# Expert stage: TensorE enters a chunk's second products after six of eight activations

## The chip, the cores and the metric

The kernel runs on one core of one Trainium2 chip. The metric is the device time of one execution in microseconds (us). The time before is the median of three runs.

## What is computed

A graph network, a slice attention block, a hypergraph convolution and a mixture of experts are applied one after the other to 3125 nodes of 256 features, each added to its input. Only the last of them is touched:

```
logits = xt @ Wr + br
weights, top_idx = the two largest of softmax(logits), made to sum to 1
xe = xn[None, :, :] * ln_g[:, None, :] + ln_b[:, None, :]
h = jax.nn.gelu(jnp.einsum('end,edh->enh', xe, W1) + b1[:, None, :], approximate=False)
y = jnp.einsum('enh,ehd->end', h, W2) + b2[:, None, :]
out = (weights[:, :, None] * sel).sum(axis=1)
```

There are 8 experts, 256 features and a hidden width of 1024. `sel` are the outputs of a node's two experts.

## The kernel before, and its expert stage

The five engines run queues of their own and meet at semaphores. TensorE (PE) multiplies, ScalarE (ACT) applies the gelu, VectorE (DVE) scales and adds, GpSimd (POOL) issues the indirect transfers of rows, and SyncE (SP) issues the loads of weights.

**Chunks.** The pairs of node and expert are sorted by expert into 32 chunks: 24 of two units of 128 rows (256 rows) and 8 of one unit (128 rows). They are done in 8 turns of `TURN` = 4 chunks, three of two units and then one of one unit. Seven turns stand in a hardware loop (line 2475), where the values that semaphores are compared with are worked out in registers. The eighth is written out (line 2477) with constant values.

**What TensorE does for a chunk.** `turn_rows` (line 2431) transposes the gathered rows of the next chunk: four transposes for two units, two for one unit. `outputs` (line 2449) makes the second products of the present chunk. `hidden` (line 2439) makes the first products of the next chunk: 8 hidden blocks of 128 rows (`EK` = 8), each the sum of two matmuls, into PSUM banks 0 to 3 in turn. Each fp32 matmul shows as two weight loads (PEld) and two matmuls in the trace, so `hidden` is 32 of each, and `outputs` is 32 for two units and 16 for one. `turn_of_chunks` (line 2462) puts the three in the order `turn_rows`, `outputs`, `hidden`. The last chunk has no `turn_rows` before its `outputs`.

**The activations.** ScalarE (line 1057) reads each finished hidden block from PSUM, applies the gelu and writes block k of `hT`, then adds 1 to `e_gelu` (named `expert_gelus` where the order is shown). `outputs` loads block k of `hT` as the weights of product k, for k from 0 to 7, once for each unit i. `hidden` waits for `e_gelu` before it writes a bank again, at k = 4 to 7. The buffers `hT`, the weights `w1e` and `w2e` and the rows `xin` are double.

**Around it.** VectorE scales the transposed rows (line 1885, `xeT`) and later adds the bias and the gate to the output (lines 1893 and 1894), which adds 1 to `e_y`. GpSimd then adds the rows to `x_sum` by an indirect transfer (line 738) and gathers the rows of the chunk three further on (line 723, `xin`). SyncE loads W1 of the chunk two further on once all gelus of the present one are done (line 551), and its W2 (line 557) once the present output is made.

Line 2451 is the wait of `outputs` for the gelus:

```
pe.wait_ge(w2e_in[s], wi)
pe.wait_ge(e_gelu, gelu)
pe.wait_ge(e_y, y)
```

Of the kernel before, what the change touches and what calls it, by code (L numbers as in the profile page):

```python
# [61 lines left out]
EK = EH // P  # L62
# [44 lines left out]
def build(nc, x, src, dst, w, out):  # L107
    ctx = ExitStack()
    with ctx:
# [223 lines left out]
        def fresh(tag, *names):  # L333
            return [sem(f"{tag}_{n}") for n in names]
# [25 lines left out]
        e_tps, e_xe, e_hps, e_gelu, e_yps, e_y = fresh("expert", "transposed", "inputs", "hidden", "gelus", "outputs", "rows_out")  # L360
# [1550 lines left out]
        def _(pe):  # L1911
# [536 lines left out]

            def outputs(gelu, y, wi, s, n):
                pe.wait_ge(w2e_in[s], wi)  # L2450
                pe.wait_ge(e_gelu, gelu)
                pe.wait_ge(e_y, y)
                for i in range(n):
                    for k in range(EK):
                        ins = M(ps[:, 4 + s, i * F:(i + 1) * F], hT[s][:, k, i * P:(i + 1) * P], w2e[s][:, k, :], start=(k == 0), stop=(k == EK - 1))  # L2455
                ins.then_inc(e_yps, 1)

# [4 lines left out]
            def turn_of_chunks(g, last):  # L2462

                for j in range(TURN):
                    s, n, m = j % 2, UNITS_OF[j], UNITS_OF[(j + 1) % TURN]
                    final = last and j == TURN - 1
                    if not final:
                        turn_rows(rows_of(g, j + 1), 1 - s, m)
                    outputs(g * (TURN * EK) + (j * EK + EK + 1), g * TURN + (j + 1), g * (TURN * 16) + (j // 2 * 32 + 32), s, n)
                    if not final:  # L2470
                        hidden(g * (TURN * 2) + (2 * j + 4), g * (TURN * EK) + (j * EK + EK + 1), g * (TURN * 8) + ((j + 1) // 2 * 16 + 16), 1 - s, m)
# [28 lines left out]
```

## Time and profile before

| | us |
|---|---|
| median of three runs | 2862.1 |
| lowest and highest of them | 2860.65, 2863.26 |
| the profiled execution | 2860.8 |
| its span, first to last instruction | 2858.9 |
| TensorE matmul busy in the span | 2384.4 (83%) |

The profile comes from one execution of 2860.8 us, which is 1.9 us longer than its span and 1.3 us under the median. The expert stage fills the last 440 us of the span, from about 2419 us on. A timeline row has the start, the length, the engine with its line, the operation and how many instructions were merged; in square brackets stands how long the engine was idle before it and what the profile names as what ended that. "issue" means that the profile shows nothing it waited for. A weight load and its matmul overlap, and the ends of matmuls are modelled, so the rows of PEld tell best when TensorE goes on.

### The profile page before, as it was taken

The numbers are of one execution on the slowest core, as the hardware profiler recorded it, in microseconds if no ns is written. First come the engines' busy times: TensorE is split into PE (matmuls) and PEld (weight loads), VectorE is DVE, ScalarE is ACT, GpSimd is POOL, SyncE is SP. The second block draws the span as 40 slices with busy tenths as digits, with TensorE's granted clock in tenths as the row PEclk, the third lists the DMA queues.
The fourth block names the chain that finished last, engine by engine and source line by source line (L and its number), as shares of the span: only waits on it lengthen the run. The fifth ranks groups of instructions, "written<-read, shape, count | busy, mean of one in ns | idle before, by whom it ended". The sixth has DMA issues, their size and how long they took to land.

```text
span 2858.9 us, 39637 instructions
## 1 busy us (share of the span) xinstructions
PE 2384.4 (83%) x14320; PEld 1787.8 (63%) x14320; DVE 1037.8 (36%) x2746; ACT 450.0 (16%) x1221; POOL 881.8 (31%) x651
## 2 busy tenths in 40 slices
PE   5285553577859999999997888999999995999997
PEld 2151111345547776777774457888888895888886
DVE  7688885243321011112125745112220456111111
ACT  0030000000015000004104822000110002222222
POOL 6888888888830000000003410000000001333332
PEclk6595555798979999999999979999999996999999
DMA  9922223876460999990253000444344434667665
GB/s 338 311 1 0 0 1 63 236 207 184 68 192 0 215 224 243 238 246 0 81 165 107 1 1 1 138 147 133 124 143 154 158 124 147 192 200 216 198 202 171
DMA packets 298592, 397.88 MB, mean 139 GB/s; under 512 B 178133, under 2 KB 242028, under 8 KB 298410
## 3 DMA queue, kind: packets, MB, share of 16 engines
q1 hardware_dynamic: 115530, 268.24, 29.5%
q10 hardware_dynamic: 110560, 108.20, 14.3%
q0 software_dynamic: 72400, 20.05, 8.3%
q8 instruction: 67, 1.10, 0.2%
q14 instruction: 35, 0.29, 0.0%
HBM read 279.31 MB, written 99.82 MB: 133 GB/s over the span
## 4 chain that ended last, share of the span: by engine, by line
PE 63%; POOL 15%; DVE 7%; issue 6%; DMA 5%; ACT 1%; ACTq 1%; DVEq 0%; SPq 0%; POOLq 0%
PE ps L2045 14%; PE ps L2359 9%; PE ps L2361 9%; POOL odd_counts L617 7%; POOL at_counts L617 7%; PE ps L2455 7%; PE ps L2446 6%; PE ps L1971 4%; DMA odd_counts<-tarena 3%; PE ps L2063 3%; DVE late L1219 2%; PE ps L2292 2%; PE ps L2176 2%; PE ps L2315 2%; PE ps L2222 1%
## 5 line engine op out<-in xcount | busy, mean ns | idle before, releaser
L2359 PE MATMUL ps<-harena,ring 128*128 128x257 f16 (+1 forms) x2500 | 540.3, 272 | 5.1 <-DVE harena L1688 3.7
L2361 PE MATMUL ps<-harena,ring 128*128 128x256 f16 x2400 | 534.4, 271 | 0.0
L2045 PE MATMUL ps<-ring,harena 128*128 128x320 f16 (+1 forms) x3740 | 506.2, 297 | 1.4 <-ACT tarena L815 0.8
L2045 PEld LDWEIGHTS ps<-ring,harena 128*128 128x128 f16 x3740 | 366.8, 98 | 137.6 <-issue 3.1
L617 POOL DMA_INDIRECT at_counts<-harena x208 | 327.8, 1576 | 81.6 <-issue 78.3
L617 POOL DMA_INDIRECT odd_counts<-harena x208 | 330.1, 1587 | 66.7 <-issue 61.3
L1219 DVE SCALAR_TENSOR_TENSOR late<-ps,ring 128x512 f16<-128x512 f32 x416 | 287.4, 746 | 22.0 <-PE ps L1933 11.2
L1933 PE MATMUL ps<-harena,ident 104*128 104x512 f32 x208 | 186.6, 1014 | 116.3 <-DVE late L1219 115.3
L2359 PEld LDWEIGHTS ps<-harena,ring 128*128 128x128 f16 x2500 | 243.2, 97 | 40.1 <-DVE harena L1688 5.9
L2361 PEld LDWEIGHTS ps<-harena,ring 128*128 128x128 f16 x2400 | 232.2, 97 | 29.9
L685 POOL IOTA harena<- 1x32 int32 x1 | 0.2, 184 | 709.4 <-DVE xrows L1770 709.4
L2455 PE MATMUL ps<-ring,harena 128*128 128x256 f32 x896 | 201.7, 382 | 9.4 <-ACT harena L1057 5.2
L1933 PEld LDWEIGHTS ps<-harena,ident 104*128 104x128 f32 x208 | 50.3, 286 | 246.1 <-DVE late L1219 230.7
L2446 PE MATMUL ps<-harena,ring 128*128 128x256 f32 (+1 forms) x1024 | 201.7, 356 | 1.2 <-DVE harena L1885 1.2
L2455 PEld LDWEIGHTS ps<-ring,harena 128*128 128x128 f32 x896 | 167.6, 190 | 38.1 <-issue 16.5
L2446 PEld LDWEIGHTS ps<-harena,ring 128*128 128x128 f32 x1024 | 177.2, 192 | 22.3 <-issue 1.6
L2063 PE MATMUL ps<-feat,wl 128*128 128x320 f32 x448 | 130.4, 452 | 63.9 <-DVE feat L1301 47.0
L738 POOL DMA_INDIRECT x_sum<-harena x56 | 88.8, 1586 | 267.3 <-DVE harena L1894 227.5
L1057 ACT ACTIVATE harena<-ps,harena 128x256 f32<-128x256 f32 (+1 forms) x256 | 114.6, 448 | 310.1 <-PE ps L2446 302.1
L786 ACT ACTIVATE bn_k<-bn_k 128x4 f32<-128x4 f32 (+1 forms) x3 | 0.6, 204 | 1026.7 <-DMA at_counts<-ring 620.5
L2063 PEld LDWEIGHTS ps<-feat,wl 128*128 128x128 f32 x448 | 88.0, 199 | 104.5 <-issue 50.1
L1301 DVE SCALAR_TENSOR_TENSOR feat<-ps,sc,late 128x640 f32<-128x640 f32 x30 | 26.5, 884 | 340.6 <-PE ps L2045 340.6
(410 smaller groups left out, 2486.3 us busy)
## 6 DMA issues: line engine op xcount, KB each, us to landing
ring<-at_counts SPq DMA_DIRECT2D x145, 800.0 KB
ring<-L_ffn_W SPq DMA_DIRECT2D x64, 1024.0 KB, 5.2
ring<-ad_counts SPq DMA_DIRECT2D x50, 800.0 KB
at_counts<-tarena ACTq DMA_DIRECT2D x5, 4000.0 KB, 21.8
odd_counts<-tarena ACTq DMA_DIRECT2D x5, 4000.0 KB
ad_counts<-xrows ACTq DMA_DIRECT2D x25, 800.0 KB, 7.8
xrows<-odd_counts SPq DMA_DIRECT2D x20, 800.0 KB
at_counts<-ring ACTq DMA_DIRECT2D x20, 800.0 KB
```

Source lines behind the costliest of these rows:

```text
L617: nc.gpsimd.indirect_dma_start(out=table, out_offset=bass.IndirectOffsetOnAxis(ap=eidx[:, c:c + 1], axis=0), in_=evalue[:, c:c + 1], in_of ...
L738: nc.gpsimd.indirect_dma_start(out=x_sum, out_offset=bass.IndirectOffsetOnAxis(ap=to_row[:, j:j + 1], axis=0), in_=yrow[c % 2][:, i, :], i ...
L1057: nc.scalar.activation(hT[s][:, k, 0:n], ps[:, k % 4, 0:n], ACT.Gelu, bias=evc[s][:, k:k + 1]).then_inc(e_gelu, 1)
L1219: ins = V.scalar_tensor_tensor(out=ejunk[q], in0=ps[:, LOOK + s, :], scalar=ekey[:, bass.ds(g + q, 1)], in1=eweight[:, GE - P - q * P:2 * ...
L1933: M(ps[:, LOOK + g % LOOK, :], ident[0:ER, g:g + 1].to_broadcast([ER, P]), ekeyT, start=True, stop=True).then_inc(keys_spread, 1)
L1971: ins = M(ps[:, 4 + n % 4, 0:c], weights[:, d, fo * P:(fo + 1) * P], feat[:, d, h * HB:h * HB + c], start=(d == 0), stop=(d == 3))
L2045: ins = M(ps[:, 2 * f + h, 0:c], part[:, t, (2 * k + f) * P:(2 * k + f + 1) * P], chunk[q][:, s, h * HB:h * HB + c], start=(t == 0 and par ...
L2063: ins = M(ps[:, k + h, 0:HB], wl2[:, d, fo * P:(fo + 1) * P], feat[:, d, h * HB:(h + 1) * HB], start=(d == 0), stop=(d == nfi - 1))
L2359: ins = M(ps[:, i, 0:wide], lhs, hh[:, t, 0:wide], start=(t == 0), stop=(t == T - 1))
L2361: ins = M(ps[:, i, 0:F], lhs, hl[:, t, :], start=False, stop=False)
L2446: ins = M(ps[:, k % 4, 0:n * P], w1e[s][:, d, k * P:(k + 1) * P], xeT[s][:, d, 0:n * P], start=(d == 0), stop=(d == 1))
L2455: ins = M(ps[:, 4 + s, i * F:(i + 1) * F], hT[s][:, k, i * P:(i + 1) * P], w2e[s][:, k, :], start=(k == 0), stop=(k == EK - 1))
```

## The change

`outputs` no longer asks for all eight gelus of its chunk before its first product. It asks for six, and then, in the first unit's pass alone, for the seventh before product k = 6 and for the eighth before product k = 7. The products, their order and their operands are the same. `gelu` counts all eight, so `gelu - EK + 1 + k` is `gelu - 1` at k = 6 and `gelu` at k = 7.

```diff
             def outputs(gelu, y, wi, s, n):
                 pe.wait_ge(w2e_in[s], wi)
-                pe.wait_ge(e_gelu, gelu)
+                pe.wait_ge(e_gelu, gelu - 2)
                 pe.wait_ge(e_y, y)
                 for i in range(n):
                     for k in range(EK):
+                        if i == 0 and k >= EK - 2:
+                            pe.wait_ge(e_gelu, gelu - EK + 1 + k)
                         ins = M(ps[:, 4 + s, i * F:(i + 1) * F], hT[s][:, k, i * P:(i + 1) * P], w2e[s][:, k, :], start=(k == 0), stop=(k == EK - 1))
                 ins.then_inc(e_yps, 1)
```

The other engines' instructions are the same. On TensorE, in the loop, this is the third chunk of a turn, after the two transposes for the chunk of one unit. A row is an instruction, with the semaphores that it waits for; REGISTER_ALU works out a value in a register, and may carry a wait itself.

```order
 L2451 REGISTER_ALU [waits expert_W2_in0]
 L2452 REGISTER_ALU [waits expert_gelus]
-L2455 MATMUL ps<-ring,harena 128x256 [waits expert_rows_out]
-L2455 MATMUL ps<-ring,harena 128x256 x15
+L2457 MATMUL ps<-ring,harena 128x256 [waits expert_rows_out]
+L2457 MATMUL ps<-ring,harena 128x256 x5
+L2456 REGISTER_ALU
+L2457 MATMUL ps<-ring,harena 128x256 [waits expert_gelus]
+L2456 REGISTER_ALU
+L2457 MATMUL ps<-ring,harena 128x256 [waits expert_gelus]
+L2457 MATMUL ps<-ring,harena 128x256 x8
```

The wait at the entry stays and asks for a smaller value, and two waits and two register computations stand between the 6th and the 8th product (in two of the four chunks of a turn it is one computation). On TensorE in the turn that is written out, from the end of `hidden` of the last chunk to the end of the stage, before:

```order
 L2446 MATMUL ps<-harena,ring 128x128 [waits expert_gelus]
 L2446 MATMUL ps<-harena,ring 128x128
 L2455 MATMUL ps<-ring,harena 128x256 [waits expert_rows_out,expert_gelus,expert_W2_in1]
 L2455 MATMUL ps<-ring,harena 128x256 x7
```

and with the change:

```order
 L2446 MATMUL ps<-harena,ring 128x128 [waits expert_gelus]
 L2446 MATMUL ps<-harena,ring 128x128
 L2457 MATMUL ps<-ring,harena 128x256 [waits expert_rows_out,expert_gelus,expert_W2_in1]
 L2457 MATMUL ps<-ring,harena 128x256 x5
 L2457 MATMUL ps<-ring,harena 128x256 [waits expert_gelus] x2
```

Here no register is worked out, and the two further waits sit on the last two products.

## Rows read from the trace of the kernel before

**Rows 1.** The page: the span, and the last chain by engine.

```profile
span 2858.9 us, 39637 instructions
...
PE 63%; POOL 15%; DVE 7%; issue 6%; DMA 5%; ACT 1%; ACTq 1%; DVEq 0%; SPq 0%; POOLq 0%
```

**Rows 2.** Windows: stretch, length, busy time by engine, granted clock, DMA share, GB/s.

```profile
2530.00:2585.00 55.00, 53.83 (x269) 47.04 (x268) 8.72 (x16) 15.92 (x36) 19.63 (x15) 1.00 0.73 216
```

**Rows 3.** Waits of weight loads from 2420 us: who for whom, total, times, longest.

```profile
PEld ps L2455 <- issue: 16.5, 31, 0.7
...
PEld ps L2436 <- DMA harena<-xn_rows,harena: 0.6, 1, 0.6
```

**Rows 4.** Timeline, entry of `outputs` after four transposes, a chunk of two units.

```profile
2534.72 0.57 PEld L2436 LDWEIGHTS ps<-ident,harena 128*128 128x128 f32 x4
...
2535.20 0.48 ACT L1057 ACTIVATE harena<-ps,harena 128x256 f32<-128x256 f32 x1 [0.39 <-PE ps L2446]
...
2535.80 0.19 PEld L2455 LDWEIGHTS ps<-ring,harena 128*128 128x128 f32 x1 [0.50 <-issue]
2535.80 0.48 PE L2455 MATMUL ps<-ring,harena 128*128 128x256 f32 x1 [0.27 <-ACT harena L1057]
```

**Rows 5.** Timeline, entry after two transposes, a chunk of two units.

```profile
2460.33 0.47 ACT L1057 ACTIVATE harena<-ps,harena 128x256 f32<-128x256 f32 x1 [0.39 <-PE ps L2446]
...
2460.93 0.30 PEld L2455 LDWEIGHTS ps<-ring,harena 128*128 128x128 f32 x2 [0.71 <-issue]
```

**Rows 6.** Timeline, entry after four transposes, the chunk of one unit.

```profile
2471.77 0.37 ACT L1057 ACTIVATE harena<-ps,harena 128x128 f32<-128x128 f32 x1
...
2472.26 0.30 PEld L2455 LDWEIGHTS ps<-ring,harena 128*128 128x128 f32 x2 [0.39 <-issue]
```

**Rows 7.** Timeline, the last chunk, and the last addition of rows.

```profile
2835.74 1.71 ACT L1057 ACTIVATE harena<-ps,harena 128x128 f32<-128x128 f32 x4
...
2837.52 3.32 PEld L2455 LDWEIGHTS ps<-ring,harena 128*128 128x128 f32 x16 [0.72 <-issue]
...
2842.44 1.55 POOL L738 DMA_INDIRECT x_sum<-harena  x1 [3.88 <-DVE harena L1894]
```

**Rows 8.** Timeline, the second turn's start, where the gathered rows come late.

```profile
2482.99 0.47 ACT L1057 ACTIVATE harena<-ps,harena 128x256 f32<-128x256 f32 x1 [0.39 <-PE ps L2446]
2483.06 0.42 PEld L2436 LDWEIGHTS ps<-ident,harena 128*128 128x128 f32 x4 [0.57 <-DMA harena<-xn_rows,harena]
...
2483.59 0.30 PEld L2455 LDWEIGHTS ps<-ring,harena 128*128 128x128 f32 x2
```

**Rows 9.** Timeline, weight loads of whole `outputs` and `hidden` groups.

```profile
2519.94 3.76 PEld L2446 LDWEIGHTS ps<-harena,ring 128*128 128x128 f32 x32
...
2535.80 6.77 PEld L2455 LDWEIGHTS ps<-ring,harena 128*128 128x128 f32 x32 [0.50 <-issue]
...
2542.59 6.88 PEld L2446 LDWEIGHTS ps<-harena,ring 128*128 128x128 f32 x32
```

**Rows 10.** Timeline of SP and POOL at a turn's end: loads and gather.

```profile
2522.01 0.37 SPq L557 DMA_DIRECT2D ring<-L_ffn_W  x1
...
2525.32 0.29 SPq L551 DMA_DIRECT2D ring<-L_ffn_W  x1
...
2527.28 0.99 POOL L723 DMA_INDIRECT harena<-xn_rows,harena  x1 [0.30 <-issue]
...
2529.35 0.37 SPq L557 DMA_DIRECT2D ring<-L_ffn_W  x1
```

**Rows 11.** Windows: the ten microseconds around that gather.

```profile
2525.00:2535.00 10.00, 10.00 (x48) 8.75 (x47) 1.30 (x3) 3.32 (x7) 4.28 (x4) 1.00 1.03 326
```

**Rows 12.** The last chain in order of time: the late rows of the second turn.

```profile
2475.09 7.94 DMA harena<-xn_rows,harena
```

**Rows 13.** The page, DMA issues: out, in, count, KB each, median us to landing.

```profile
ring<-L_ffn_W SPq DMA_DIRECT2D x64, 1024.0 KB, 5.2
```

**Rows 14.** The page, groups: instructions, count, busy us, mean ns, idle before.

```profile
L2455 PE MATMUL ps<-ring,harena 128*128 128x256 f32 x896 | 201.7, 382 | 9.4 <-ACT harena L1057 5.2
```

## The prediction

> **What bounds the kernel now.** I read the page first. The span is 2858.9 us, and the chain that ended last lies on TensorE for 63% of it [rows 1]. The change touches the last 440 us alone, so the next view is the busy time by stretch. From 2530 to 2585 us matmuls are busy 53.83 of 55 us, the granted clock is 1.00, the upper of the two levels (2.4 GHz), and the DMA engines are busy 0.73 of the time [rows 2]. TensorE sets the pace there, and what it idles is worth its full length, since the tail after it (output, addition, store) is released by it.
>
> The third view is the list of waits. TensorE's weight loads of `outputs` waited 31 times, 16.5 us in all [rows 3]. The profile puts this down to "issue", so it names no cause. The timeline of one entry gives it. The four weight loads of the transposes start at 2534.72 and end at 2535.29. The eighth gelu runs from 2535.20 to 2535.68. The first weight load of `outputs` starts at 2535.80, after 0.50 us idle and 0.12 us after the gelu's end [rows 4]. The same 0.12 to 0.13 stands in the other forms: gelu end 2460.80, load 2460.93, idle 0.71 [rows 5]; gelu end 2472.14, load 2472.26, idle 0.39 [rows 6]. Even where the transposes themselves came late, the gelu ends at 2483.46 and the load starts at 2483.59 [rows 8]. In the written-out turn, with no register to work out, it is 0.07 (2837.45 to 2837.52) after an idle time of 0.72 [rows 7]. So the eighth gelu is what every entry waits for. It is short of cover: it ends about 0.6 us after `hidden`'s last product, and four short transposes fill only part of that.
>
> **Part 1, the entry wait falls from eight gelus to six.** Gelus of a chunk of two units follow each other every 0.87 us (0.48 busy, 0.39 idle) [rows 4], so the sixth ends 1.73 us before the eighth, at about 2533.95. That is 0.8 us before the transposes begin. In a chunk of one unit four gelus take 1.71 us [rows 7], 0.43 each, so the sixth of the last chunk ends at about 2836.59, and 0.07 later is 2836.66, still before the 2836.80 at which its load group has ended (2837.52 less 0.72). So the entry wait no longer ends last anywhere. What does is TensorE's own queue. The other two entry waits, W2 and the output buffer, aren't near: the tightest W2 is issued at 2522.01 and read at 2535.80, 13.8 us later [rows 10, 4], against a median landing of 5.2 us [rows 13] and the 7.94 us of the late rows [rows 12]. The output buffer was freed a chunk ago.
>
> Taken back: the 31 idle times, **16.5 us** [rows 3]. Four transposes' loads start 0.11 us apart and last 0.14 (0.57 us for four whose first step is 0.22) [rows 4]. A next load would thus start some 0.03 us before the last one's end, which adds 31 x 0.03, **0.9 us**.
>
> **Part 2, two new waits per chunk.** Behind each stands everything TensorE has left to do, and VectorE's output addition waits for the end of it. Product 6 is the 13th weight load of `outputs`. At 0.216 us each (31 steps and 0.19 in 6.88 us [rows 9]) it comes 2.6 us after the entry. With the entry at about 2535.27 that is 2537.9, and the eighth gelu ends at 2535.68 [rows 4]: 2.2 us of cover, worth nothing saved or lost while the gelus keep their pace. If that cover were gone, each us that a gelu ends later would cost a us. For one unit the margin is the same 2.6 us less at most 0.7 [rows 7].
>
> What does a wait that is already satisfied cost in the middle of a stream? `hidden` has four of them in each group, most with a register computation, and no step shows: 32 loads in 6.88 us at 256 columns, and 32 in 3.76 us at 128, where there would be least to hide them behind. The group `outputs`, with no wait inside, took 6.77 us, which is 0.11 less, but its second load comes 0.11 early because the first had waited [rows 9]. So the lower bound is zero. The upper bound for a wait is 0.05 us, the difference between the two lags after the gelu (0.12 with a register computation, 0.07 without) [rows 4, 7]: 64 x 0.05 = 3.2 us. I take **zero**, because `hidden` is the same pattern on the same engine.
>
> The seam itself: does TensorE go from the last transpose to the first product without a pause when the waits are satisfied? From `outputs` to `hidden`, also past register computations and two waits, it does: the one group ends at 2542.57 and the next starts at 2542.59 [rows 9]. If the 0.12 us of a released wait stayed at each entry, 32 x (0.12 + 0.03) = 4.8 us would be lost. I take none, and keep it for the range.
>
> **Part 3, what is late next: the rows of a turn's second chunk.** They are gathered at the turn's end, beside two 1 MB weight loads, with the DMA engines at 1.03 of their time and 326 GB/s [rows 10, 11]. The gather starts at 2527.28 and its rows are transposed at 2534.72, 7.44 us later [rows 10, 4]. In the second turn they needed 7.94 us [rows 12], and the transposes waited 0.57 us, the only such wait [rows 3]. It cost nothing then, since the gelu came last anyhow. Between that gather and those transposes lies one entry, that of the chunk of one unit, so the room falls by 0.39 + 0.03 = 0.42 us to 7.02. In the second turn the rows are then the bound. The load that now starts at 2483.59 could start 0.11 after the transposes' last, at 2483.45, which is 0.14 us sooner [rows 8]. From gather to `outputs` it gains 0.14 where the other terms counted 0.42 (the entry itself had no idle time in the 16.5): **-0.3 us**. For the six other turns I only know that the rows took at most 7.44 us. Some may need more than 7.02, the more so as the next W2 (issued 2529.35 [rows 10]) starts 0.42 us sooner and shares the engines. Bounds: 0, or 0.42 in each, 2.5 us. I take **-0.3 us**, one late turn.
>
> **The sum.** 16.5 + 0.9 - 0 - 0.3 - 0.3 = 16.8 us. The profiled execution would go from 2860.8 to 2844.0, and the median from 2862.1 to **2845.3 us**, 0.6% less. A measurement of this kernel can tell about 0.2%, 5.7 us, from no change. The end of the span moves with TensorE, since the last addition of rows was released by the last output (its idle time of 3.88 us ended with VectorE) [rows 7].
>
> **A page that speaks against it.** The Trainium skill (Advanced Engine Details and Errata, section Network/Comms) says that reading a semaphore from the sequencer takes 50 to 100 ns on trn2. If each of the 64 new waits paid that on TensorE's path, an estimate from that page, 3.2 to 6.4 us of the gain would go, and the sum would be 10.4 to 13.6. `hidden`'s even steps [rows 9] speak against it; it is rival 2 below.
>
> **The rivals.**
>
> 1. *The rows come late in every turn.* For: in the second turn it is so already, and the DMA engines are full there [rows 11, 12]. Against: in six of seven turns nothing waited for rows [rows 3]. Price: if all seven need 7.94 us, each turn has only 0.14 of the 0.95 us that it could have between gather and `outputs` (0.42 and 0.53). The sum without any lateness is 16.5 + 0.9 + 0.5 = 17.9, less 7 x 0.81 = 5.7: 12.2 us, **2849.9**.
>
> 2. *A satisfied wait costs 0.05 us in mid-stream*, by the difference of the lags [rows 4, 7]. 16.8 - 3.2 = 13.6 us, **2848.5**. Against it stand the steps of `hidden`.
>
> 3. *Each new wait empties TensorE's pipeline.* After a real wait the first matmul shows 0.48 us, where the mean over all of them is 0.38, so about 0.10 is lost beside the lag of 0.12 [rows 4, 14]. 64 x 0.22 = 14.1 us, leaving 2.7: **2859.4**, which is within 0.2%. Against: again `hidden`, and that the gelus are done 2.2 us before.
>
> 4. *The change doesn't do what it says.* "issue" could mean that TensorE's own queue needs the 0.5 us for three register computations, and the gelu's end falls beside it by chance. Then nothing is gained, and 0 to 3.2 us of new computations are lost: **2862.1 to 2865.3**. Against: the idle time is 0.39, 0.50 and 0.71 by form while the distance to the gelu stays at 0.12 [rows 4 to 6], and the 0.72 stands where no register is worked out [rows 7].
>
> 5. *Slower: a W2 load gets in front of the gathered rows.* Place: the turn's end. W2 of the turn's second chunk is issued 2.07 us after the gather now [rows 10] and 0.42 sooner with the change. Its 1 MB at 326 GB/s [rows 11] is 3.2 us, which the rows would land later in each of seven turns. 17.9 - 7 x 3.2 would be -4.5 us, and with the 0.42 us less room up to -7.4: **2866.6 to 2869.5**. It decides from rows that need 7.0 + 3.4 = 10.4 us, because only then are 7 x 3.4 us lost, the whole 17.9 and the 5.7 of a visible loss. The longest seen is 7.94 [rows 12].
>
> **How the numbers follow.** Forecast 0.78, rival 1 0.08, rival 2 0.05, rival 3 0.03, rival 4 0.03, rival 5 0.03. Faster by over 0.2% are the forecast and rivals 1 and 2: 0.91. Within 0.2% are rivals 3 and 4: 0.06. Slower: 0.03. The range takes in the forecast and rivals 1 and 2. Its low end is the sum without lateness, 2862.1 - 17.9 = 2844.2, less the 1.4 us by which the lowest run lies under the median: 2842.8. Its high end is rival 1 at 2849.9, about what the 4.8 us of a lag at each entry would give too (2850.1), with a little of the runs' spread: 2850.8.
>
> **What the changed profile would show.** Right: the 16.5 us of waits before `outputs`' weight loads gone or under 1 us; the first load of `outputs` 0.03 us before the transposes' last one has ended; `outputs` in even steps of 0.216 us past the 12th load; a turn of about 50.0 us instead of 52.2 (2483.59 to 2535.80 [rows 8, 4]); the eighth gelu ending inside `outputs`. Part 3 shows as waits of the transposes for gathered rows, once or twice, at the start of a turn. Wrong: a step over 0.25 us at the 13th or 15th load (rivals 2 and 3), an entry that still starts 0.12 us after something (the seam), or waits for rows in every turn (rivals 1 and 5).

## The result, and the profile after

| | before | after |
|---|---|---|
| first six runs of each, median | 2862.7 us | 2844.0 us |
| ratio, 95% interval | | 0.9927 (0.9897 to 0.9956) |
| later set, 12 runs against 35, median | 2863.1 us | 2845.8 us |
| ratio, 95% interval | | 0.9940 (0.9917 to 0.9964) |
| profiled execution | 2860.8 us | 2842.3 us |
| its span | 2858.9 us | 2840.5 us |

The kernel is faster by 0.6 to 0.7%. The forecast was 2845.3 us, which is 0.6%. The first ratio, set against the 2862.1 us from which the forecast started, gives 2841.2 us, which is 1.6 us below the low end of the stated range. The medians of those same runs are only 18.7 us apart, and the median of after and the later ratio (2844.9 us) lie inside. Both intervals are wide: the later one stands for 10.3 to 23.8 us, which holds the forecast and rival 1 alike. So the runs' times show that the kernel is faster, and the profiles have to show why. What was wrong is taken up behind the experiments.

The page of after, and its busy time by stretch, answer to [rows 1, 2, 11]. TensorE's matmuls are now busy 55.00 of 55 us, where it was 53.83.

```profile
span 2840.5 us, 39679 instructions
PE 64%; POOL 16%; issue 6%; DVE 6%; DMA 5%; ACTq 1%; ACT 1%; DVEq 0%; SPq 0%; POOLq 0%
```

```profile
2530.00:2585.00 55.00, 55.00 (x280) 48.94 (x279) 9.72 (x18) 14.77 (x33) 20.02 (x17) 1.00 0.76 219
2520.00:2530.00 10.00, 10.00 (x49) 8.76 (x48) 1.61 (x4) 3.31 (x7) 4.56 (x4) 1.00 1.02 325
```

The waits of weight loads from 2420 us on, which answer to [rows 3], are down to a single row. It is the first `hidden` of the stage, which also stood there before. The 16.5 us before `outputs` are gone.

```profile
PEld ps L2446 <- issue: 1.6, 1, 1.6
```

The timeline of after (line 2457 is the product that was line 2455) shows the entries that answer to [rows 4 to 8]: behind four transposes and behind two, the chunk of one unit, the last chunk, and the starts of the first and the second turn.

```profile
2529.62 0.58 PEld L2436 LDWEIGHTS ps<-ident,harena 128*128 128x128 f32 x4
2530.10 0.47 ACT L1057 ACTIVATE harena<-ps,harena 128x256 f32<-128x256 f32 x1 [0.39 <-PE ps L2446]
2530.16 6.78 PEld L2457 LDWEIGHTS ps<-ring,harena 128*128 128x128 f32 x32
...
2458.12 0.36 PEld L2436 LDWEIGHTS ps<-ident,harena 128*128 128x128 f32 x2
2458.45 0.73 PEld L2457 LDWEIGHTS ps<-ring,harena 128*128 128x128 f32 x4
2458.60 0.47 ACT L1057 ACTIVATE harena<-ps,harena 128x256 f32<-128x256 f32 x1 [0.39 <-PE ps L2446]
...
2468.85 0.81 ACT L1057 ACTIVATE harena<-ps,harena 128x128 f32<-128x128 f32 x2
2469.36 0.52 PEld L2457 LDWEIGHTS ps<-ring,harena 128*128 128x128 f32 x3
...
2430.16 6.78 PEld L2457 LDWEIGHTS ps<-ring,harena 128*128 128x128 f32 x32
...
2480.16 1.38 PEld L2457 LDWEIGHTS ps<-ring,harena 128*128 128x128 f32 x7
...
2818.94 3.33 PEld L2457 LDWEIGHTS ps<-ring,harena 128*128 128x128 f32 x16
```

Three things can be read from it. `outputs` starts at 2530.16, before the transposes' loads have ended (2530.20), and the eighth gelu now runs inside `outputs`, from 2530.10 to 2530.57. The group of 32 loads with two waits in it takes 6.78 us, where the group without them took 6.77. And a turn lasts 50.00 us (2430.16 to 2480.16, again to 2530.16), where it lasted 52.21.

The sharpest measure of the change is the stretch from the first entry of `outputs` to the last. I call it the chunk stage. Before, it begins here and ends at 2837.52 [rows 7]:

```profile
2431.38 0.30 PEld L2455 LDWEIGHTS ps<-ring,harena 128*128 128x128 f32 x2 [0.50 <-issue]
```

That is 406.14 us before and 388.78 us after, 17.36 us less. The span shrank by 18.4. Of the other 1.0 us, 0.5 are the first entry's own idle time, which lies ahead of that stretch, and the rest is in parts that the change does not touch: the first transposes, for one, start at 2418.68 us and not at 2419.13.

### The profile page after: what moved, and what is told of

The parts are those of the page before. It is cut to its first block, busy times and chain, and to the rows that moved or that the text cites. A ratio compares the mean times of both kernels' runs of the same rounds, so it can differ in the third digit from the quotient of the medians.

```text
span 2840.5 us, 39679 instructions
## 1 busy us (share of the span) xinstructions
PE 2374.6 (84%) x14320; PEld 1785.8 (63%) x14320; DVE 1038.2 (37%) x2746; ACT 449.4 (16%) x1221; POOL 881.4 (31%) x651
## 4 chain that ended last, share of the span: by engine, by line
PE 64%; POOL 16%; issue 6%; DVE 6%; DMA 5%; ACTq 1%; ACT 1%; DVEq 0%; SPq 0%; POOLq 0%
PE ps L2045 14%; PE ps L2359 9%; PE ps L2361 9%; POOL odd_counts L617 8%; POOL at_counts L617 8%; PE ps L2446 7%; PE ps L2457 7%; PE ps L1971 4%; DMA odd_counts<-tarena 4%; PE ps L2063 3%; PE ps L2292 2%; PE ps L2176 2%; PE ps L2315 2%; PE ps L2222 1%; DVE late L1219 1%
```

## Experiments

All are compared by their chunk stage, in one profiled execution each, since whole runs spread far more (see the end of this part). Where a kernel was also timed in several runs beside the kernel before, the ratio stands beside it; experiments 5, 6 and 7 have the profiled execution alone. Two things recur below. A turn with no late rows lasts 50.00 us in the profile of after. And gathered rows that come late show as a wait of the transposes (line 2436), in the second turn alone as long as no fill delays them; the first such wait, of about 6 us, stands ahead of the stage's first chunk in every run and is not part of the chunk stage.

**1. The change once more.** No edit.

> The changed kernel unaltered, in five rounds. The question is whether its gain of 0.73% (18.7 us between the medians) is more than the forecast 16.8 us. Theory A (the chunk stage gives 17.9 us, all that the entries had, and no row came late; anything beyond is other stages' spread): chunk stage, from the first to the last entry of outputs, again 388.8 us against 406.1, the time from the span's start to the first transposes anywhere within 2 us of 2418.7 to 2419.1, ratio 0.9930 to 0.9945. Theory B (the change also speeds up something outside the chunk stage, by 1 to 3 us): the first transposes again at 2418.7 or earlier while the kernel before keeps 2419.1, ratio 0.9920 to 0.9930.

Measured: median 2845.8 us in 12 runs, ratio 0.9940 (0.9917 to 0.9964). Timeline, the first transposes, the first and the last entry, and then the wait of transposes:

```profile
2419.70 0.72 PEld L2436 LDWEIGHTS ps<-ident,harena 128*128 128x128 f32 x4 [5.89 <-DMA harena<-xn_rows,harena]
...
2431.40 0.30 PEld L2457 LDWEIGHTS ps<-ring,harena 128*128 128x128 f32 x2
...
2820.36 0.52 PEld L2457 LDWEIGHTS ps<-ring,harena 128*128 128x128 f32 x3
```

```profile
PEld ps L2436 <- DMA harena<-xn_rows,harena: 0.4, 1, 0.4
```

The chunk stage is 388.96 us, 0.18 more than in the first profile. The second turn's rows came late here, and its transposes waited 0.4 us. The first transposes start at 2419.70 us, 0.6 later than in the kernel before, so this profile shows no gain ahead of the stage. The ratio is theory A's, though its interval takes in theory B's too: it is the profile that decides.

**2. A wait before every product.** 352 waits more than in the change.

```diff
-                        if i == 0 and k >= EK - 2:
+                        if i > 0 or k > 0:
                             pe.wait_ge(e_gelu, gelu - EK + 1 + k)
```

> The changed kernel with a wait before every product of outputs, each for the gelu of its own block (15 per chunk of two units, 7 per chunk of one, instead of 2), nearly all with a value worked out in a register; 13 x 24 + 5 x 8 = 352 waits more. Theory A (a satisfied wait costs TensorE nothing in mid-stream): as the changed kernel, 2843 to 2846 us, loads of outputs in steps of 0.216 us. Rival 2 (0.05 us each): 17.6 us more, 2861 to 2863 us. Rival 3 (0.22 us each): 77 us more.

Measured: median 2847.7 us, which is 1.7 us over the range expected for whole runs; ratio 0.9938 (0.9911 to 0.9965). Timeline and waits:

```profile
2440.24 0.52 PEld L2457 LDWEIGHTS ps<-ring,harena 128*128 128x128 f32 x3
...
2490.43 0.42 PEld L2436 LDWEIGHTS ps<-ident,harena 128*128 128x128 f32 x4 [0.75 <-DMA harena<-xn_rows,harena]
2490.81 1.17 PEld L2457 LDWEIGHTS ps<-ring,harena 128*128 128x128 f32 x6
...
2540.82 6.78 PEld L2457 LDWEIGHTS ps<-ring,harena 128*128 128x128 f32 x32
...
2829.59 0.30 PEld L2457 LDWEIGHTS ps<-ring,harena 128*128 128x128 f32 x2
```

```profile
PEld ps L2436 <- DMA harena<-xn_rows,harena: 7.1, 2, 6.3
```

32 loads with 15 waits among them take 6.78 us, as with two. The stage is 389.35 us, 0.57 more than in the change, and all of it lies in the first turn (2440.24 to 2490.81, 50.57 us), at whose end the rows of the second were 0.75 us late. Each of the six turns behind it lasts 50.00 us (2490.81 to 2540.82 and so on), as in the change, with 44 waits more in each. Rivals 2 and 3 asked for 17.6 and 77 us more. A satisfied wait cost nothing, register computation included.

**3. The change in the chunks of one unit alone.**

```diff
-                pe.wait_ge(e_gelu, gelu)
+                pe.wait_ge(e_gelu, gelu - (2 if n == 1 else 0))
...
+                        if n == 1 and k >= EK - 2:
+                            pe.wait_ge(e_gelu, gelu - EK + 1 + k)
```

> The change in the 8 chunks of one unit alone; the 24 chunks of two units wait for all eight gelus at the entry. Theory A, a sum over entries: 7 x 0.42 + 0.80 = 3.7 us under the kernel before, less nothing for late rows, since the entry behind them still has 0.5 us of cover: chunk stage 402.4 us between first and last entry. If the gains of entries did not add up (something else takes over once several are gone) this run and the rest of the change would not make up 17.4 us.

Measured: ratio 0.9973 (0.9946 to 1.0). Timeline and waits:

```profile
2451.66 0.51 PEld L2457 LDWEIGHTS ps<-ring,harena 128*128 128x128 f32 x3 [0.50 <-issue]
...
2854.08 0.30 PEld L2457 LDWEIGHTS ps<-ring,harena 128*128 128x128 f32 x2
```

```profile
PEld ps L2457 <- issue: 13.4, 24, 0.7
PEld ps L2436 <- DMA harena<-xn_rows,harena: 6.1, 2, 5.8
```

The stage is 402.42 us, against 402.4 expected. The 24 entries of two units keep their idle time, 13.4 of the 16.5 us. Rows were late by 0.3 us at one turn and cost nothing, because the gelu still covered them. The gains of entries add up.

**4. Entering after seven gelus.**

```diff
-                pe.wait_ge(e_gelu, gelu - 2)
+                pe.wait_ge(e_gelu, gelu - 1)
...
-                        if i == 0 and k >= EK - 2:
+                        if i == 0 and k == EK - 1:
```

> The changed kernel, entering outputs after seven gelus and waiting for the eighth before product 7 alone: 32 waits fewer than the change. Theory A: the seventh gelu ends 0.87 us before the eighth and so before the transposes' end in chunks of two units, which keep everything; a chunk of one unit has its seventh gelu 0.44 us before its eighth, so with the lag of 0.12 its entry comes about 0.1 us later than with six, and the last one about 0.35 us: 7 x 0.1 + 0.35 = 1 us slower than the changed kernel in the chunk stage. Rival 2 (0.05 us per wait): 32 x 0.05 = 1.6 us faster than the changed kernel.

Measured: ratio 0.9948 (0.9915 to 0.9980). Timeline and waits:

```profile
2433.43 0.52 PEld L2457 LDWEIGHTS ps<-ring,harena 128*128 128x128 f32 x3
...
2823.81 0.30 PEld L2457 LDWEIGHTS ps<-ring,harena 128*128 128x128 f32 x2 [0.28 <-issue]
```

```profile
PEld ps L2436 <- DMA harena<-xn_rows,harena: 6.6, 2, 5.9
```

The stage is 390.38 us, 1.60 over the change. A late row at the second turn (a wait of 0.76 us) is 0.6 of it. The rest, 1.0 us, is what the seventh gelu was expected to cost, 0.28 of idle time at the last entry among it. That there were 32 waits fewer brought nothing. So the second of the two gelus that the change frees is worth only 1.0 us of its 17.9, all of it at the chunks of one unit.

**5. Both waits moved up to product 1.**

```diff
-                        if i == 0 and k >= EK - 2:
-                            pe.wait_ge(e_gelu, gelu - EK + 1 + k)
+                        if i == 0 and k == 1:
+                            pe.wait_ge(e_gelu, gelu)
```

> The changed kernel with one wait, for all eight gelus, moved from products 6 and 7 up to product 1. Theory A (a wait costs only what of the gelu is not yet over when it is reached): product 1's first load stands 0.33 us after the entry; the eighth gelu and the lag of 0.12 end 0.53 us after the entry behind four transposes (0.20 lost, 16 times, 15 of them in the loop with the lag of 0.12), 0.75 after it behind two (0.42 lost, 8 times), 0.41 for a chunk of one unit (0.08 lost, 7 times): 7.1 us more in the chunk stage than the changed kernel's 388.8, so about 396. If it costs as much as the kernel before (406.1), entering early is not what gained. Rival 4 (the entry's idle time is TensorE's own): 388.8, no loss.

Measured, timeline and then waits:

```profile
2432.27 0.30 PEld L2457 LDWEIGHTS ps<-ring,harena 128*128 128x128 f32 x2
2432.73 6.34 PEld L2457 LDWEIGHTS ps<-ring,harena 128*128 128x128 f32 x30 [0.16 <-ACT harena L1057]
...
2460.60 0.30 PEld L2457 LDWEIGHTS ps<-ring,harena 128*128 128x128 f32 x2
2461.28 6.34 PEld L2457 LDWEIGHTS ps<-ring,harena 128*128 128x128 f32 x30 [0.38 <-issue]
...
2823.77 0.30 PEld L2457 LDWEIGHTS ps<-ring,harena 128*128 128x128 f32 x2
```

```profile
PEld ps L2436 <- DMA harena<-xn_rows,harena: 6.4, 2, 5.8
PEld ps L2457 <- ACT harena L1057: 3.0, 16, 0.5
PEld ps L2457 <- issue: 2.8, 8, 0.4
```

The stage is 391.50 us, 2.7 over the change where 7.1 was expected. Of the 2.7 us, 0.5 are a late row at the second turn (a wait of 0.65 us), so the moved wait cost some 2.25. There are 24 stalls, at the entries behind four and behind two transposes (but for the one that follows the late row) and in the last chunk. Their cost was mis-stated twice. The third load starts 0.46 us after the entry, not 0.53, so the lag behind the gelu is nearer 0.05 than 0.12. And not all of the lateness stays. At 2432.73 the third load is 0.13 us late, and the group then ends at 2439.07, 6.80 us after its entry, where it took 6.78 in the change: 0.02 us late. At 2461.28 it is 0.35 us late, and the group lasts 7.02 us: 0.24 late. In both forms the group makes up 0.11 us of the lateness. What lets the loads catch up was not tried. In a turn's three chunks of two units that makes 0.61 us of lateness and 0.28 of cost, and turns without a late row last 50.29 us. Rival 4 is out, since moving the wait brings part of the idle time back, at the size that the gelu's end and this catching up give.

**6. The rows of a turn's second chunk made late, in the changed kernel.** GpSimd fills unused columns before that gather.

```diff
                     pool.wait_ge(e_tps, c + 2)
+                    if c % TURN == TURN - 2:
+                        o.mark(nc.gpsimd.memset(harena[:, 11008:11008 + 1800], 0.0))
+                        o.settle()
                     gather_rows(c + 3)
```

> The changed kernel; GpSimd fills 1800 unused columns (a memset, waited for) ahead of the gather of a turn's second chunk, seven times, so that these rows land later by the length d of that fill, about 1.5 to 2 us. Theory A (after the change the rows' arrival is 0.1 to 1.3 us from being the bound in every turn): each turn loses what d exceeds its spare time by. The spare times in the changed kernel's trace are 0.10, 0.58, 0.50, 0.63, 0.83, 0.99 and 1.25 us, so for d = 2 the chunk stage is 9.1 us longer, about 398, and transposes wait for rows in all seven turns. If rows were far from the bound: 388.8.

Measured. Lines are three further on: 2439 are the transposes, 2460 the second products.

```profile
2431.12 0.52 PEld L2460 LDWEIGHTS ps<-ring,harena 128*128 128x128 f32 x3
...
2521.81 2.18 POOL L743 MEMSET harena<- 128x1800 f32 x1
2524.26 1.03 POOL L723 DMA_INDIRECT harena<-xn_rows,harena  x1 [0.27 <-POOL harena L743]
...
2582.61 0.42 PEld L2439 LDWEIGHTS ps<-ident,harena 128*128 128x128 f32 x4 [1.39 <-DMA harena<-xn_rows,harena]
2583.00 0.52 PEld L2460 LDWEIGHTS ps<-ring,harena 128*128 128x128 f32 x3
...
2823.13 0.52 PEld L2460 LDWEIGHTS ps<-ring,harena 128*128 128x128 f32 x3
```

```profile
PEld ps L2439 <- DMA harena<-xn_rows,harena: 4.5, 7, 1.4
```

The stage is 392.01 us, 3.2 more than the change, where 9.1 was expected. Transposes wait for rows in all seven turns, as theory A said. The fill lasts 2.18 us and starts beside the last addition's issue, so it moves the gather only about 1.6 us nearer to its transposes. For d = 1.6 the spare times give 6.3 us of waiting. The waits sum to 4.5, so rows that were asked for later took 0.26 us less each; that they then meet less of the two weight loads beside them is my reading and was not tried. And of the 4.5 us of waiting the stage lost 3.2. This has a pattern: each of the seven turns is longer by its wait less 0.18 us (the longest wait, 1.39 us, made a turn of 51.21), and 7 x 0.18 is the 1.3 us that is missing. Four transposes' loads take 0.42 us after a wait, where they took 0.57 behind `hidden`, and `outputs` starts 0.39 us after the first of them (2582.61 to 2583.00), not 0.54.

**7. The same fill in the kernel before.**

> The kernel before, with the same fill ahead of the same seven gathers. Theory A: the room is 0.42 us longer there and 0.53 us of lateness hides behind the gelu at the entry, so for d = 2 the seven turns lose 1.9, 0.5, 0, 0.85, 0.4, 0 and 0.3 us: 3.9 us more than 406.1, about 410, less than half of what the changed kernel loses. If the change had not used up that cover, both would lose the same.

Measured (second products on line 2458 here):

```profile
2431.95 0.51 PEld L2458 LDWEIGHTS ps<-ring,harena 128*128 128x128 f32 x3 [0.50 <-issue]
...
2838.26 0.30 PEld L2458 LDWEIGHTS ps<-ring,harena 128*128 128x128 f32 x2 [0.72 <-issue]
```

```profile
PEld ps L2458 <- issue: 16.3, 31, 0.7
PEld ps L2439 <- DMA harena<-xn_rows,harena: 1.2, 2, 0.8
```

The stage is 406.31 us, 0.2 more than without the fill, where 3.9 was expected. Two waits for rows, 1.2 us in all, show, and the gelu hides nearly all of them. The same disturbance costs 0.2 us before the change and 3.2 after it. This is the price of the change that part 3 of the prediction named: the cover is gone.

**8. The gather first.** GpSimd gathers the rows three chunks on before it waits for the present output.

```diff
             for c in range(CHUNKS):
+                if c + 3 < CHUNKS:
+                    pool.wait_ge(e_tps, c + 2)
+                    gather_rows(c + 3)
                 pool.wait_ge(e_y, c + 3)
...
-                if c + 3 < CHUNKS:
-                    pool.wait_ge(e_tps, c + 2)
-                    gather_rows(c + 3)
```

> The changed kernel with GpSimd's gather of the rows of the chunk three further on ahead of its wait for the present output and the addition of its rows, instead of behind them. The gather of a turn's second chunk then starts some 12 us sooner. Theory A: no transposes wait for rows, in no turn; chunk stage 388.8 us, 0.2 to 0.6 less than runs of the changed kernel with a late turn (388.96, 389.35), too little to show in the time of whole runs: 2843 to 2847 us. Against it: the additions of rows start after gathers and could come later, which only matters if VectorE then waits for an output buffer, 7 us away.

Measured: median 2845.2 us, ratio 0.9946 (0.9923 to 0.9969). Timeline:

```profile
2430.22 0.30 PEld L2457 LDWEIGHTS ps<-ring,harena 128*128 128x128 f32 x2
...
2511.39 1.02 POOL L723 DMA_INDIRECT harena<-xn_rows,harena  x1 [4.20 <-DMA x_sum<-harena]
...
2819.00 0.30 PEld L2457 LDWEIGHTS ps<-ring,harena 128*128 128x128 f32 x2
```

The gather that began at 2521.26 in the change begins at 2511.39, 9.9 us sooner where some 12 were expected. No transposes wait for rows, and the stage is 388.78 us, the same as in the profile of after and the least seen. The 0.2 to 0.6 us that a late row costs do not show in whole runs, so this kernel is not shown to be faster. But it gives the cover back: by the landings in the trace, the rows of a turn's second chunk now lie ready 13.6 to 14.0 us before their transposes, where they had 0.1 to 1.3 us in the change, and the chunk stage is no longer for it.

**Where whole runs spread.** The 35 runs of the kernel before lie between 2857.5 and 2887.2 us. The profile of experiment 3 happens to be a long one (2877.2 us). Its first transposes start 20.3 us later than before (2439.42 against 2419.13), so the excess is ahead of the expert stage. Windows and timeline of that profile show most of it as one stall near 1070 us:

```profile
1000.00:1100.00 100.00, 80.01 (x488) 56.68 (x487) 13.61 (x23) 0.17 (x1) 0.00 (x0) 0.91 1.10 197
```

```profile
1084.63 5.69 PE L2063 MATMUL ps<-feat,wl 128*128 128x320 f32 x15 [18.40 <-ACT amax L910]
```

and the same window of the kernel before, where TensorE idled for only 1 us:

```profile
1000.00:1100.00 100.00, 98.98 (x624) 70.18 (x622) 18.12 (x37) 0.17 (x1) 0.00 (x0) 1.00 1.09 233
```

The DMA share is the same in both (1.10 and 1.09), but they moved 197 GB/s in the one and 233 in the other. The profile puts the end of the stall down to ScalarE (line 910), which itself had waited for a transfer. Why this takes longer in some executions was not tried.

## Why the prediction was right, and what was wrong

- **What bounds.** Right. All 31 idle times went, and every entry follows TensorE's own queue. Experiment 5 brought part of them back by the wait's place alone.
- **Part 1, 16.5 + 0.9 us.** Right, to the overlap of 0.03 us at the seam. The prediction's figure for a run with no late row was 17.9 us, these 17.4 and the 0.5 that the second turn's entry gives when its rows are in time. In the profile of after they were: the chunk stage lost 17.36 us and the first entry 0.5, which is 17.9.
- **Part 2, zero for the new waits.** Right. Experiment 2 multiplied them and found nothing. The page that spoke against it (the Trainium skill, Advanced Engine Details and Errata, section Network/Comms, 50 to 100 ns per read of a semaphore) does not describe a cost on TensorE's path here: by that figure, an estimate, 352 further waits would have added 17.6 to 35 us.
- **Part 3, -0.3 and -0.3 us for late rows.** Right in mechanism and in place, the second turn, and mis-sized. The room between gather and transposes did fall to 7.0 us. But in the profile of after the second turn's rows took 6.9, so the term was +0.5 us there and not -0.6. In experiment 1 they came late and the stage lost 0.2 of the 17.9, in experiments 2 and 4 it lost 0.6. The six other turns, for which 0.3 was taken, lost nothing in any of these.
- **The rivals.** Rival 1 is out for the change as it is: but for the fills of experiments 6 and 7, no run had more than one late turn. Experiments 6 and 7 show that it was a real danger and at what size. Rivals 2 and 3 fell with experiment 2, and rival 4 with the result and with experiment 5. Rival 5 needed rows that take 10.4 us from their gather, and in no trace did any take more than the 7.94 of the kernel before.
- **The step that failed is the low end of the range.** It is the sum without lateness, 17.9 us, less a run-to-run part of 1.4 us. That part was read from three runs that happened to lie within 2.6 us, as was the statement that a measurement can tell 0.2%. Six runs of each kernel left an interval of 0.6% in the ratio, some 17 us (a gain of 12.6 to 29.5), one of the six of the kernel before being 11 us over their median, and 35 runs of it spread over 30 us. The first ratio of 0.9927 asks for 20.9 us, 3 us more than the chunk stage gave in any profile; with more runs it came to 0.9940, which is 17.2. So the excess is put down to spread of other stages: no profile shows a gain of the change outside the chunk stage and its first entry, though one profile for each set of runs can't show where every run lost its time. Part 3's term is a second and smaller miss, 1.1 us in the profile of after, and with it alone the measured time would have stayed in the range. That the forecast of 16.8 us is so near the later 17.2 is in part luck, with an interval of 10.3 to 23.8. What the profiles bear out is 17.9, and 17.3 to 17.7 with one late turn. The room below the forecast should have been several us wider.

## What to carry to other kernels

When the profile puts an idle time down to "issue", look at what other engines finish just before it ends: a distance that stays the same (0.12 us here) while the idle time varies by form names the releaser. A wait for a whole group can be split and each piece put where its data is read; on TensorE the pieces cost nothing once they are satisfied. Then look for what the old wait was hiding, here gathered rows that the change left with 0.1 to 1.3 us to spare, and move that earlier as well, as experiment 8 does. Before a range is drawn from the spread of a few runs, take more of them: three runs lay within 2.6 us, 35 within 30.

## What was unexpected of the hardware

- TensorE took 15 waits, most with a value worked out in a register, within 32 weight loads of 0.216 us each and lost nothing (6.78 us).
- A weight load that is late costs less than its lateness, by an amount that stayed the same. A wait for rows ahead of four transposes cost its length less 0.18 us: 0.36 us cost 0.18 in experiment 1, 0.75 cost 0.57 in experiment 2, and so in each of the seven late turns of experiment 6. A late third load of `outputs` cost its lateness less 0.11 us in experiment 5: 0.13 us cost 0.02, and 0.35 cost 0.24.
- The rows of a turn's second chunk took 5.8 to 6.9 us from the start of their last gather to their landing in the change, where the DMA share is 1.00 (2522 to 2529 us, 312 GB/s). In experiment 8, which gathers them some 10 us sooner, at a DMA share of 0.67 (2510 to 2516 us, 220 GB/s), they took 2.9 to 3.5 us.
